# Change flags in registers, and a loop's turn at another place: a routed two-layer adapter kernel on one core

## The reference

```python
h = einsum('bsh,bhk->bsk', x, W_down[role]) + b_down[role]     # 1024 -> 512
h = gelu(h, approximate=False)
u = einsum('bsk,bkh->bsh', h, W_up[role]) + b_up[role]         # 512 -> 1024
y = x + u
y = (y - mean(y)) * rsqrt(var(y) + 1e-5) * gamma[role] + beta[role]
```

## Time and profile before

| | us |
|---|---|
| median of 3 runs | 2846.38 (2836.21 to 2849.52) |
| profiled execution | 2837.71 |
| its span, first to last instruction | 2835.8 |
| PE busy | 2713.0 (96%) |
| DVE busy | 2084.8 (74%) |
| ACT busy | 1682.4 (59%) |
| POOL busy | 1348.3 (48%) |
| mean granted TensorE clock | 0.985 of full speed |

### The profile page before, as it was taken

One profiled execution on the slowest core, in us unless ns is written; L12 is line 12 of the kernel. 1 busy time (PEld: TensorE's weight loads), 2 busy tenths in 40 slices (PEclk: granted clock), 3 DMA queues, 4 the chain that ended last, 5 costly groups with the idle time before them and its releaser, 6 DMA issues.

```text
span 2835.8 us, 58851 instructions
## 1 busy us (share of the span) xinstructions
PE 2713.0 (96%) x11714; PEld 2216.1 (78%) x11714; DVE 2084.8 (74%) x3358; ACT 1682.4 (59%) x2905; POOL 1348.3 (48%) x1050
## 2 busy tenths in 40 slices
PE   8999999988999999999989999999889999999996
PEld 5887788867788888888768787878667877878785
DVE  6677776767676767767787777777787777777776
ACT  4556656555566565666556565666556565556564
POOL 1455554544454555545444444444344444444445
PEclk9999999999999999999999999999999999999998
DMA  6656556556565665656756566666656665666663
GB/s 217 208 200 205 199 199 211 198 203 210 198 204 206 205 212 194 208 196 214 238 184 221 183 215 199 199 206 204 229 172 208 206 204 188 210 200 202 197 198 142
DMA packets 360623, 573.63 MB, mean 202 GB/s; under 512 B 40144, under 2 KB 239952, under 8 KB 359248
## 3 DMA queue, kind: packets, MB, share of 16 engines
q1 hardware_dynamic: 359136, 554.92, 59.4%
q10 hardware_dynamic: 1008, 14.68, 1.3%
HBM read 364.97 MB, written 204.47 MB: 201 GB/s over the span
## 4 chain that ended last, share of the span: by engine, by line
issue 30%; PE 24%; DVE 19%; DVEq 11%; ACT 7%; POOL 6%; ACTq 2%; POOLq 1%; DMA 0%; SPq 0%
PE pD L503 12%; DVEq L236 10%; PE bX L515 7%; PE bZ L515 5%; DVE xt L914 5%; ACT xh L626 5%; DVE hl L896 4%; POOL rstd L432 2%; DVE xT L867 2%; DVE xt L937 2%; POOL cs L459 2%; ACT pC L684 1%; DVE xt L906 1%; ACTq L236 1%; DVE wul L821 1%
## 5 line engine op out<-in xcount | busy, mean ns | idle before, releaser
L449 POOL TENSOR_TENSOR xt<-xt,cgb 128x1024 f32<-128x1024 f32 x258 | 629.6, 2441 | 433.9 <-ACT xt L692 433.9
L503 PE MATMUL pD<-wdh,xh 128*128 128x512 f32 x2080 | 817.5, 393 | 16.2 <-DVEq L858 16.2
L503 PE MATMUL pD<-wdl,xh 128*128 128x512 f32 x2080 | 815.4, 392 | 0.0
L503 PE MATMUL pD<-wdh,xl 128*128 128x512 f32 x2080 | 814.3, 391 | 0.0
L503 PEld LDWEIGHTS pD<-wdh,xh 128*128 128x128 f32 x2080 | 394.7, 190 | 103.9 <-DVEq L858 15.3
L503 PEld LDWEIGHTS pD<-wdh,xl 128*128 128x128 f32 x2080 | 394.0, 189 | 82.9
L503 PEld LDWEIGHTS pD<-wdl,xh 128*128 128x128 f32 x2080 | 394.4, 190 | 82.2
L457 POOL TENSOR_TENSOR cs<-hT 128x256 f32<-128x256 f32 x130 | 97.5, 750 | 744.7 <-DVE hT L881 744.7
L515 PE MATMUL bX<-wuh,hh 128*128 128x512 f32 x1040 | 412.7, 397 | 39.8 <-ACT bX L651 20.2
L674 ACT ACTIVATE hh<-cs 128x512 fp32r<-128x512 f32 x260 | 163.7, 630 | 482.6 <-issue 259.7
L684 ACT ACTIVATE pC<-xt,nmean 128x512 f32<-128x512 f32 x520 | 357.7, 688 | 126.8 <-DVE nmean L922 118.3
(11 more groups left out here) (106 smaller groups left out, 3800.4 us busy)
## 6 DMA issues: line engine op xcount, KB each, us to landing
xq<-in_xB SPq DMA_DIRECT2D x130, 512.0 KB, 3.5
htok<-hg SPq DMA_DIRECT2D x260, 256.0 KB, 2.5
hq<-htok SPq DMA_DIRECT2D x1040, 64.0 KB, 2.2
xt<-in_x SPq DMA_DIRECT2D x130, 512.0 KB, 4.2
mid<-xt SPq DMA_DIRECT2D x130, 512.0 KB, 3.5
xq<-mid SPq DMA_DIRECT2D x520, 128.0 KB, 3.2
xt<-mid SPq DMA_DIRECT2D x130, 512.0 KB, 4.3
out<-xt SPq DMA_DIRECT2D x128, 512.0 KB, 3.0
```

The costliest lines, as they stand in the source:

```text
L449: eng.tensor_tensor(xt[:, k, :], xt[:, k, :], cgb[:, 1, :], ALU.add).then_inc(s_o, 1)
L503: last = eng.matmul(pD[e][:, :], a[:, e, 128 * k:128 * k + 128], w[:, k, :], start=False, stop=(k == 7 and n == 2), skip_group_check=True)
```

## The change

1. `c_near` and `c_far` are joined to one table `c_kind` (0: no change, 1: far, 2: near). A step reads one entry into a register (`Kinds.read`: ScalarE two steps ahead, VectorE and SyncE one step ahead, GpSimd at once), in six registers by turns; `when_new`, `when_far` and `when_near` test the register.
2. VectorE's loops turn behind the mean that follows the sixth eviction: `begin` holds all up to there. They turn in steps 9, 15, ..., 57 and 74, 80, ..., 122.
3. In VectorE's order the low part of h's second group (`low_h(w, 1)`) goes from between the scaling and the fourth eviction to behind the turn. `onto(u, 1)` goes ahead of `take_wd_1`.
4. `take_wu_0` is split: the bias subtraction (`bias`, with `s_cb` raised) goes ahead of `low_x(i + 1, 0)`; the low parts of blocks 0 and 1 stay, with `s_wu[0]`; those of 2 and 3 and the subtraction behind them (`take_wu_1`, new `s_wu[1]`) follow the seventh eviction. `factors` (far) and `s_wd[0]` stand behind the seventh eviction too; TensorE waits for three up-weight semaphores (products 0 and 1, 2 and 3, 4 to 6).
5. ScalarE's tests and issues of the weight loads go behind its loop's turn; its `take_wd_0` goes from ahead of `seed_d` to behind the seeds of `bX` and `bZ`, and the wait for the down bias stands alone ahead of `seed_d`.

```diff
@@ steps, when @@
-            for first in (behind, NP + 5):
+            for first in (behind, NP + back):
...
-                with eng.If(eng.value_load(flags[0:1, bass.ds(p.times(1), 1)], min_val=0, max_val=1) == 1):
+            def read(self, p):
+                if p.exists():
+                    self.eng.reg_load(self.regs[p.c % M], c_kind[0:1, bass.ds(p.times(1), 1)])
+            def when_far(self, p, do):
+                if p.exists() and not p.first():
+                    with self.eng.If(self.eng.snap(self.regs[p.c % M]) == 1):
+                        do(p)
...
@@ tensor @@
-                    count(eng, s_wu[n // 4], u, 1, 1)
+                    count(eng, s_wu[min(n // 2, 2)], u, 1, 1)
@@ scalar @@
             def begin(i):
-                when_new(eng, i, take_wd_1)
+                kinds.read(i + 2)
+                kinds.when_new(i, take_wd_1)
...
-                when(eng, c_near, i + -2, load_up)
-                when(eng, c_far, i, load_up)
-                when(eng, c_near, i + 1, load_down)
-                when(eng, c_far, i + 2, load_down)
             def end(i):
                 u, w = i + -3, i + -2
+                kinds.when_near(w, load_up)
+                kinds.when_far(i, load_up)
+                kinds.when_near(i + 1, load_down)
+                kinds.when_far(i + 2, load_down)
                 high_h(w, 1)
...
-                when_new(eng, i + 1, take_wd_0)
+                kinds.when_new(i + 1, bias_landed)
                 seed_d(i + 1, 0)
                 normal(u + -1, 1)
                 seed_x(w)
                 seed_z(w)
+                kinds.when_new(i + 1, take_wd_0)
                 square(u, 0, 0)
@@ vector @@
             def begin(i):
                 u, w = i + -3, i + -2
...
+                kinds.read(i + 1)
                 transpose_h(w, 0)
                 transpose_h(w, 1)
-                when_new(eng, i, take_wd_1)
+                onto(u, 1, X, 0, 0)
+                kinds.when_new(i, take_wd_1)
                 ready(i, s_wd[1])
-                onto(u, 1, bX[u.c % 2], 0, 0)
                 low_x(i, 1)
                 onto(u, 2, bZ, 1, 1)
                 low_h(w, 0)
...
                 onto(u, 3, X, 0, 1)
-                when_new(eng, u, take_wu_2)
-                ready(u, s_wu[1])
+                kinds.when_new(u, take_wu_2)
+                ready(u, s_wu[2])
...
                 scale(u + -1, 0)
                 scale(u + -1, 1)
-                low_h(w, 1)
                 last_onto(u, 4, bZ, 0, 1, 3)
                 transpose_x(i + 1, 0)
                 last_onto(u, 5, X, 1, 1, 2)
+                kinds.when_new(w, bias)
+                ready(w, s_cb)
                 low_x(i + 1, 0)
                 last_onto(u, 6, bZ, 0, 0, 1)
                 mean(u, 0, 6)
-                when(eng, c_new, w, take_wu_0)
-                ready(w, s_cb)
+
+            def end(i):
...
+                low_h(w, 1)
+                transpose_x(i + 1, 1)
+                kinds.when_new(w, take_wu_0)
                 ready(w, s_wu[0])
-                transpose_x(i + 1, 1)
-                when(eng, c_far, i + -1, factors)
-                when_new(eng, i + 1, take_wd_0)
-                ready(i + 1, s_wd[0])
                 low_h(w, 2)
-                last_onto(u, 7, X, 1, 0, None)
+                last_onto(u, 7, bX[u.c % 2], 1, 0, None)
                 mean(u, 1, 7)
+                kinds.when_far(i + -1, factors)
+                kinds.when_new(w, take_wu_1)
+                ready(w, s_wu[1])
+                kinds.when_new(i + 1, take_wd_0)
+                ready(i + 1, s_wd[0])
                 low_h(w, 3)
...
-            steps(eng, halves(begin, end), -1, NPH + 5, 0, 5)
+            steps(eng, halves(begin, end), -1, NPH + 5, 1, 4, 4)
```

More of the change, by code:

```diff
@@ L153, in routed_adapters @@
         s_wul = sem("s_wul")
-        s_wu = [sem(f"s_wu{k}") for k in range(2)]
+        s_wu = [sem(f"s_wu{k}") for k in range(3)]
         s_sub = sem("s_sub")
@@ L189, in count, with steps @@
                 eng.wait_ge(s, p.times(per, plus))
-        def steps(eng, body, low, high, ahead, behind):
-            for first in (behind, NP + 5):
+        def steps(eng, body, low, high, ahead, behind, back):
+            for first in (behind, NP + back):
                 for c in range(low, first):
@@ L231, in turned, with __init__, when_near, when_new @@
             eng.wait_ge(s_T, p.times(2, e + 1 - 2 * NP))
-        def when(eng, flags, p, do):
-            if p.exists() and not p.first():
-                with eng.If(eng.value_load(flags[0:1, bass.ds(p.times(1), 1)], min_val=0, max_val=1) == 1):
-                    do(p)
-        def when_new(eng, p, do):
-            if p.first():
-                do(p)
-            else:
-                when(eng, c_new, p, do)
+        class Kinds:
+            def __init__(self, eng, name):
+                self.eng = eng
+                self.regs = [eng.alloc_register(f"{name}{k}") for k in range(M)]
+            def read(self, p):
[5 more added lines that the diff above has]
+                        do(p)
+            def when_near(self, p, do):
+                if p.exists() and not p.first():
+                    with self.eng.If(self.eng.snap(self.regs[p.c % M]) == 2):
+                        do(p)
+            def when_new(self, p, do):
+                if p.first():
+                    do(p)
+                elif p.exists():
+                    with self.eng.If(self.eng.snap(self.regs[p.c % M]) >= 1):
+                        do(p)
         class Phases:
@@ L403, in step @@
                 if not v.first():
-                    when_new(eng, v, up_biases)
-            steps(eng, step, -1, NPH + 4, 2, 6)
+                    kinds.when_new(v, up_biases)
+            steps(eng, step, -1, NPH + 4, 2, 6, 5)
             for k in range(4):
@@ L570, in load_up, with bias_landed @@
                 fetch_up(eng, adapter(p), fu.next())
+            def bias_landed(p):
+                eng.wait_ge(s_bd, pb.next() * 16 + 16)
+                eng.sem_inc(s_seen, 1)
             def high_wd(p, c, q):
@@ L716, in end @@
                 high_h(w, 2)
-                when(eng, c_new, w, take_wu_0)
-                when_new(eng, i + 1, take_wd_0)
+                if not w.first():
+                    kinds.when_new(w, take_wu_0)
+                kinds.when_new(i + 1, bias_landed)
                 seed_d(i + 1, 0)
@@ L727, in end @@
                 square(u, 1, 1)
-            steps(eng, halves(begin, end), -1, NPH + 5, 0, 5)
+            steps(eng, halves(begin, end), -1, NPH + 5, 0, 5, 5)
         @block.vector
@@ L831, in factors, with bias, take_wu_1 @@
                 eng.tensor_tensor(t4, b21, t2, ALU.subtract).then_inc(s_sub, 1)
+            def bias(p):
+                c = pb.next()
+                eng.wait_ge(s_bu, c * 16 + 16)
+                eng.tensor_tensor(cbu[:, K:H], cbu[:, K:H], cbu[:, 0:K], ALU.subtract).then_inc(s_bz, 1)
+                eng.wait_ge(s_bz, c + 1)
+                eng.sem_inc(s_seen, 1)
             def take_wu_0(p):
                 c = pg[0].next()
-                eng.wait_ge(s_bu, c * 16 + 16)
-                eng.tensor_tensor(cbu[:, K:H], cbu[:, K:H], cbu[:, 0:K], ALU.subtract).then_inc(s_bz, 1)
                 low_wu(c * 7, 0, b11)
                 low_wu(c * 7, 1, b12)
+                eng.wait_ge(s_wul, c * 7 + 2)
+                eng.sem_inc(s_seen, 1)
+            def take_wu_1(p):
+                c = pg[1].next()
                 low_wu(c * 7, 2, t2)
@@ L964, in begin @@
                 u, w = i + -3, i + -2
-                transpose_h(w, 0)
-                transpose_h(w, 1)
-                when_new(eng, i, take_wd_1)
-                ready(i, s_wd[1])
-                onto(u, 1, bX[u.c % 2], 0, 0)
-                low_x(i, 1)
-                onto(u, 2, bZ, 1, 1)
-                low_h(w, 0)
-                if i.j is None and i.c == 2:
-                    take_wu_0(Pair(0))
-            def end(i):
-                u, w = i + -3, i + -2
                 X = bX[u.c % 2]
@@ L981, in end @@
                     return
+                kinds.read(i + 1)
+                transpose_h(w, 0)
+                transpose_h(w, 1)
+                onto(u, 1, X, 0, 0)
+                kinds.when_new(i, take_wd_1)
+                ready(i, s_wd[1])
+                low_x(i, 1)
+                onto(u, 2, bZ, 1, 1)
+                low_h(w, 0)
                 if u.last():
```

53 lines of the change are left out of this document (30 added, 23 removed).

## The result

The changed kernel takes 2803.27 us (median of 4 runs, 2795.97 to 2804.04) against 2842.9 (median of 4 runs of the kernel before, 2836.21 to 2849.52): a ratio of 0.9855, 95% interval 0.9824 to 0.9886. It is faster by 40 us, where 85 were forecast. The profiled execution spans 2801.1 us, 34.7 less than the one before; rows and tables are of these two.

A forecast was written before the change was run, and what follows sets the result against it. TensorE was taken to bound nearly every step, with 131 us lost in steps 4 to 129; 52 would remain, winning 79, plus 5.5 at the end: 2846.4 - 85 = 2761 us, range 2720 to 2806.

The forecast's parts named there:

- a sign of being wrong: Outcomes listed as refuting the forecast: turns TensorE never sees, a regular step over 20.4 us, or waits longer than t allows.
- part 2: VectorE's turn and second low part moved: matmul 60 wait goes; turns lose 25 us, 3 in layer one, 22 in layer two.
- Part 1: Flag tests become register tests, 0.2 us each: nothing won in a regular step, but the sixth eviction's mean starts about 16.0.
- The turns' own term: Stall at matmul 6 behind a turn: t - 3.1 in layer one (0.4 us), t - 2.0 in layer two (1.9 us).
- t: Length of VectorE's turn, from the mean's start to the next instruction's: taken as 3.5 us in layer one, 3.9 in layer two.
- Part 3: Weight loads behind ScalarE's turn: the 7 us that steps 28 and 93 each lose are gone.
- Part 4: Adapter changes at pairs 30, 65 and 95: 24 us still lost (15 to 38), where 78 were lost before.
- My upper bound: For the two down-weight subtractions ahead of step 33's raise, taken as 1.2 to 1.5 us: one had taken 3.36 us.
- Part 5: The end, steps 130 to 132 at VectorE's pace: 1.8 us a step won, 5.5 in all (2 to 9).
- D: Rival, chance 0.07: a register's test costs what a flag's does, adding 38 us over 18 turns: 2799.
- C: Rival, chance 0.16: adapter changes stay dear, each subtraction as long as the 3.36 us one, 38 us lost: 2784.
- E: Rival, chance 0.06: slower or no gain, the turn's fetch queues behind DMA traffic; 2836 at t = 6.4, 2850 at t = 8.

The follow-up runs named there:

- regs: The kernel before with only the change flags read into registers once a step, all else left where it was: 2755.1 us, ratio 0.9714.
- regs_issue: The kernel before with flags in registers, plus ScalarE's tests and issues of weight loads moved behind its loop turn: 2755.3 us, ratio 0.9709.

## Why the prediction was wrong in size and right in sign

- **Regular steps and layer one.** Right for layer one: nothing before matmul 60, a mean 15.9 us into the step (16.0), and turns of 0.3 to 0.4 us each (0.4). In layer two regular steps came out over 20.4 us, which the forecast had named as a sign of being wrong (part 2).
- **Part 1, "in a regular step nothing is won".** The step that failed as reasoning. It is true of a regular step, but in the step of a turn the same tests, ahead of the turn and behind it, held the fourth eviction back by 3.2 us with the low part beside them, and it was two us late. `regs` shows it: 53 us lost at the turns before (as the forecast counts them), under 2 there. I gave all of that to part 2. Then I judged the turn's new place by what it takes away, and never asked what part 1 leaves for it to win.
- **Part 2, the low part.** The step that failed here is that a step without a turn was put at nothing. The low part was sized at 0.69 us; beside GpSimd's addition it takes 2.0 in layer one and up to 2.68 in layer two. From the mean (15.9 us into the step) to the raise there are 5.9 us, since it is due at 21.8. In step 102 the second mean starts 5.2 us after the first (2178.89 less 2173.69), and the tests and the raise behind it bring it to 6.1. So the two steps ahead of each turn lose too, 0.5 and 0.6 to 1.2 us. For layer two 22 us were forecast and 32.7 measured (12.7 and 17.9, and 2.1 in step 93). The turns' own term was right: the eight steps behind them lose 18.9 us, seven of them 2.2 each, with waits that the sum gives to some tenths at t = 4.3. The rest was in no term: 11.0 us in the sixteen steps ahead of the turns, 1.6 in steps 127 to 129 and 1.2 in step 69, behind a change.
- **Part 3.** Right that ScalarE's long idleness at step 28 is cut, to 4.42 us for the 10.84 of the earlier trace rows (the longest behind a turn is 5.0, in step 93, where 3.4 were forecast):
```profile
581.16 0.63 ACT L699 ACTIVATE hh<-cs 128x512 fp32r<-128x512 f32 x1 [4.42 <-issue]
```
  But with registers and the turn at its old place it wins nothing (`regs_issue`). Registers alone had taken what it was to win: in `regs` ScalarE still idles 7.55 us at step 28, and the step loses 0.4.
- **Part 4.** The term that was mis-sized most: 24 us forecast, some 60 measured (62.3 in the three windows, less 0.3 and 2.1 for the turns of steps 28 and 93). Step 32, from 656.7, and the window of step 33 in the changed kernel:
```profile
670.96 1.55 DVE L865 TENSOR_TENSOR cbu<-cbu 128x512 f32<-128x512 f32 x1
...
674.70 0.21 DVE L959 TENSOR_SCALAR nmean<-ys 128x1 f32<-128x1 f32 x1
...
678.10 2.49 DVE L933 TENSOR_TENSOR hl<-cs,hh 128x512 fp32r<-128x512 f32 x1 [0.32 <-DVE wul L850]
...
681.24 0.21 DVE L959 TENSOR_SCALAR nmean<-ys 128x1 f32<-128x1 f32 x1
681.79 1.23 DVE L850 TENSOR_TENSOR wul<-twu,wuh 128x1024 fp32r<-128x1024 f32 x1 [0.33 <-issue]
...
678.28:709.20 30.92, 23.54 (x91) 18.06 (x90) 23.84 (x30) 16.97 (x30) 12.66 (x9) 0.89 0.42 140
```
  The bias ahead of the low x part (1.55 us and 0.3 to the next) puts the first mean at 18.0 us where 15.9 is its place, and the low h part is stretched to 2.49. So mean 7 starts at 24.5 us and not at 21.0, and the raise comes 4 us later than the 23.9 of the sum. The wait is 4.9 us for 2.1. With it, 2.4 us of other waits up to the start of step 34, and a granted clock of 0.89 over the window, step 33 loses 10.5 us, for 3.7. My upper bound took one long subtraction and left both of these at their undisturbed place and length. The turns of steps 33 and 98, at 2.3 and 4.3 us in the sum, show as waits of 2.4 and 3.4 us at matmul 0 and 6 of steps 34 and 99. The other two changes lose most elsewhere. Behind `factors` TensorE waits 2.7 us at matmul 6 of steps 67 and 97, for 0.65: in layer two a transpose of 1.25 us and a low part of 2.6 stand ahead of them. And it waits 2.8 and 3.2 us at matmul 0 of steps 68 and 98, for `s_wu[0]`, which had no term. Ahead of that raise, in steps 67 and 97, are the two subtractions of `take_wu_0`, one of them of 3.4 us:
```profile
1412.73 3.39 DVE L850 TENSOR_TENSOR wul<-rwu,wuh 128x1024 fp32r<-128x1024 f32 x1
```
  Step 67 loses 7.3 us and step 97 8.0.
- **Part 5.** 2.2 us at the end, of 5.5. The 7.4 us in two waits for the first eviction (above) are there; what makes it late I didn't try.
- **Rivals and range.** 2803 us is inside the stated range of 2720 to 2806 by 3 us, and outside the 2740 to 2780 that the forecast gave itself. The range reached so far only for D (2799), and D is refuted: registers are 85 us cheaper than flags. So the range held by luck. C's outcome (the changes stay dear) is what happened, at 60 us and not 38; its mechanism, every subtraction as long as 3.36 us, is not: only one each in steps 67 and 97 is, and the others of the three changes' up weights take 1.2. E's long fetches didn't come: the turn takes 3.1 us (layer one) to 4.6 us at the new place. That one part of the change takes back what another gives was not among them.

## What to carry to other kernels

Price each part of a change against the kernel with the other parts in it. Here one part alone was worth 85 us, and the others took 48 back. Before a signal is moved behind work, write the chain up to its due time with every instruction as long as it takes beside its new neighbours; three ways to take that chain's lateness away (a shorter neighbour, the work put back, the signal put ahead) each gave about 30 us. A signal that says "nothing changed" needs to stand behind nothing.
